# A four-layer graph network kernel on one core: a quarter of the first pass's gathers moved ahead of it, into the sort and the block build

## The reference, cut to what matters

```python
edge_feat = jnp.concatenate([h[src], h[dst]], axis=-1)
messages = _mlp2(edge_feat, msg_W1, msg_b1, msg_W2, msg_b2)
att = jax.nn.sigmoid(_mlp2(edge_feat, att_W1, att_b1, att_W2, att_b2))
weighted = messages * att
aggregated = jax.ops.segment_sum(weighted, dst, num_segments=num_nodes)
combined = jnp.concatenate([h, aggregated], axis=-1)
new_h = _mlp2(combined, upd_W1, upd_b1, upd_W2, upd_b2)
h = new_h + h + global_repr
```

## Time and profile before

| | |
|---|---|
| device time, median of 3 runs | 7433.94 us (7425.34 to 7442.86) |
| span of the profiled execution | 6780.1 us |
| the profiled execution's own time | not given by the page; the median above is 653.8 us over its span |
| busy in the span | PE 5024.0, DVE 3111.1, POOL 2431.9, ACT 1789.9 us |
| gathers of the two attention passes | 1632, 998 ns each in the mean |

### The profile page before, as it was taken

One profiled execution on the slowest core, in us unless ns is written; L12 is line 12 of the kernel. 1 busy time (PEld: TensorE's weight loads), 2 busy tenths in 40 slices (PEclk: granted clock), 3 DMA queues, 4 the chain that ended last, 5 costly groups with the idle time before them and its releaser, 6 DMA issues. The chain is left out here.

```text
span 6780.1 us, 95615 instructions
## 1 busy us (share of the span) xinstructions
PE 5024.0 (74%) x29088; PEld 3414.4 (50%) x29089; DVE 3111.1 (46%) x7292; ACT 1789.9 (26%) x4343; POOL 2431.9 (36%) x2473
## 2 busy tenths in 40 slices
PE   2557767777777777777798999999999997443443
PEld 1435556666665676666544444444444444333333
DVE  6889986666664666666565212112112114111111
ACT  2019983444443444444201001001011012000000
POOL 0000006777773777777100000000000001777776
PEclk7569998999999999999899999999999998555555
DMA  2019984444443444444483553553554524211122
GB/s 79 1 47 328 328 279 133 128 121 125 124 121 80 133 128 130 123 129 126 138 304 131 194 192 133 194 193 131 194 180 146 194 97 167 52 51 51 51 51 55
DMA packets 416540, 942.73 MB, mean 139 GB/s; under 512 B 61857, under 2 KB 272982, under 8 KB 406230
## 3 DMA queue, kind: packets, MB, share of 16 engines
q1 hardware_dynamic: 312150, 672.91, 29.4%
q0 software_dynamic: 104192, 267.02, 14.8%
HBM read 735.13 MB, written 204.56 MB: 139 GB/s over the span
## 5 line engine op out<-in xcount | busy, mean ns | idle before, releaser
L1799 POOL DMA_INDIRECT ring<-rows,stage x1632 | 1629.5, 998 | 1138.4 <-ACT stage L1846 642.0
L1677 POOL DMA_INDIRECT ring<-rows,stage x808 | 792.3, 981 | 2716.8 <-ACT stage L1661 2470.9
L1324 PE MATMUL ps<-strip,trans_part 128*128 128x512 f16 (+1 forms) x8232 | 1606.4, 356 | 23.3 <-DVE trans_part L1241 23.3
L1871 PE MATMUL ps<-here,spread 128*128 x3264 | 949.0, 414 | 545.5 <-DVE spread L1810 283.9
L1324 PEld LDWEIGHTS ps<-strip,trans_part 128*128 128x128 bf16 x8232 | 756.5, 98 | 928.2 <-issue 77.4
L1871 PEld LDWEIGHTS ps<-here,spread 128*128 128x128 f32 x3264 | 569.9, 194 | 662.2 <-issue 615.5
L1829 DVE TENSOR_TENSOR ring<-ring,ps 128x512 f32<-128x512 f32 x816 | 560.6, 687 | 699.3 <-PE ps L1871 540.9
L1728 PE MATMUL ps<-ring,mark 128*128 128x128 f32 x1616 | 414.9, 438 | 612.3 <-DMA ring<-rows,stage 610.7
L1889 PE MATMUL ps<-ring,mark 128*128 128x128 f32 x3264 | 695.0, 300 | 0.0
L1728 PEld LDWEIGHTS ps<-ring,mark 128*128 128x128 f32 x1616 | 357.3, 326 | 669.9 <-issue 669.9
L1233 DVE TENSOR_TENSOR trans<-ps,be 128x512 f32<-128x512 f32 x96 | 66.4, 692 | 1186.4 <-PE ps L1314 1186.4
(11 more groups left out here) (332 smaller groups left out, 5093.7 us busy)
## 6 DMA issues: line engine op xcount, KB each, us to landing
strip<-adj SPq DMA_DIRECT2D x392, 800.0 KB, 4.3
adj<-piece SPq DMA_DIRECT2D x120, 640.0 KB, 4.0
locs<-loc_rows SPq DMA_DIRECT2D x420, 128.0 KB, 3.1
ahead<-ahead_piece SPq DMA_DIRECT2D x125, 320.0 KB, 4.1
back<-back_piece SPq DMA_DIRECT2D x125, 320.0 KB, 4.5
sheet<-ahead SPq DMA_DIRECT2D x25, 1600.0 KB, 7.4
sheet<-back SPq DMA_DIRECT2D x25, 1600.0 KB, 7.2
ring<-rows,stage POOLq DMA_INDIRECT x2440, 2.5
```

The source lines that it names most:

```text
L1324: last = eng.matmul(k.ps[:, b, 0:cols], part[:, (step * NW + w) % TABLES, m, t * D:(t + 1) * D], strip[:, at % RING, c0:c0 + cols], start= ...
L1677: eng.indirect_dma_start(ring[:, t, :], None, rows, bass.IndirectOffsetOnAxis(stage[:, t:t + 1], 0)).then_inc(s_full[q], 16)
L1799: eng.indirect_dma_start(ring[:, t, :], None, rows, bass.IndirectOffsetOnAxis(stage[:, t:t + 1], 0)).then_inc(s_full[q], 16)
L1871: last = eng.matmul(hid[:, j, :], spread[:, q, t * P:(t + 1) * P], here[:, bass.ds(cols[t] * 2, W2)], start=True, stop=True)
```

## The change

- `layer0`'s mean phase and the first step's table become one phase, `first_rows`, which runs between `route` and `adjacency`. It stores both halves of the table to device memory (`rows0`, and `here0`, since no SBUF is free for `here` that early), and `h` as `h0`.
- In the phases of the sort, of decode and of the block build POOL gathers the first tile of each quad, four quads to a group, into six slots that lie in the buffers of `x` and `h` (`Ahead`). Three groups later it stores a group to `early_rows` in device memory with a plain DMA of 512 KB. 40 groups stand in the sort, 4 in decode, 7 in the build: 204 gathers and 51 stores.
- The first attention pass gathers three tiles of each quad. SP brings the fourth from `early_rows` and, at the pass's start, `here`, `h` and `x`. PE waits for `here` before its first `expand`.
- The loop over the two steps is unrolled; the second step still has its table phase and four gathers to a quad. `first_node` becomes the integer tile `src_no`, which is then refilled with the source numbers by one DVE copy.

```diff
+EARLY = NT // QUAD // QUAD
+AFTER_SORT, AFTER_DECODE = 40, 44
...
+                eng.tensor_copy(k.src_no[:, :], k.by_dst[:, 0:NT, D_SRC])
...
+class Ahead:
+    SLOTS, LAG = 6, 3
...
+    def fetch(self, eng):
+        n = self.end - self.first
+        def keep(i):
+            j = i % self.SLOTS
+            eng.wait_ge(self.s_got[j], 16 * QUAD * (i // self.SLOTS + 1))
+            quads = self.k.early[(self.first + i) * QUAD:(self.first + i + 1) * QUAD, :, :]
+            eng.dma_start(quads.rearrange("q p c -> p q c"), self.slots[j]).then_inc(self.s_kept[j], 16)
+
+        for i in range(n):
+            j = i % self.SLOTS
+            if i >= self.SLOTS:
+                eng.wait_ge(self.s_kept[j], 16 * (i // self.SLOTS))
+            for t in range(QUAD):
+                tile = ((self.first + i) * QUAD + t) * QUAD
+                eng.indirect_dma_start(self.slots[j][:, t, :], None, self.k.rows0,
+                                       bass.IndirectOffsetOnAxis(self.k.src_no[:, tile:tile + 1], 0)).then_inc(self.s_got[j], 16)
+            if i >= self.LAG:
+                keep(i - self.LAG)
+        for i in range(max(0, n - self.LAG), n):
+            keep(i)
+        for j in range(min(n, self.SLOTS)):
+            eng.wait_ge(self.s_kept[j], 16 * len(range(j, n, self.SLOTS)))
...
+            for to, of in loads[:1]:
+                eng.dma_start(to, of).then_inc(s_here, 16)
+            for q in range(NQ):
+                fetch(q * QUAD, q)
+                if early is not None:
+                    refill(q, q)
+            for to, of in loads[1:]:
+                eng.dma_start(to, of).then_inc(s_back, 16)
...
-                    for t in range(q * QUAD, (q + 1) * QUAD):
+                    for j in gathered:
+                        t = q * QUAD + j
...
+                    if early is not None:
+                        eng.wait_ge(s_early[q], i * 16 + 16)
...
+            @block.sync
+            def _(eng):
+                eng.dma_start(k.h0, k.h[:, :, :].rearrange("p w d -> p (w d)")).then_inc(s_h, 16)
+                for g in range(NW // G):
+                    eng.wait_ge(s_src, (g + 1) * G)
+                    eng.dma_start(of(k.rows0, g), src_st[:, g % 2, :, :]).then_inc(s_st[g % 2], 16)
+                    eng.wait_ge(s_dst, (g + 1) * G)
+                    eng.dma_start(of(k.here0, g), dst_st[:, g % 2, :, :]).then_inc(s_st[g % 2], 16)
...
-        with nc.Fori(0, 2) as _step:
+        for step in range(2):
+            if step:
...
+        first_rows(k)
```

More of the change, by code:

```diff
@@ L640, in sort_bins @@
     PERM = 4
+    ahead_rows = Ahead(k, 0, AFTER_SORT)
     with nc.Block() as block:
@@ L1748, in open_banks, with attention_pass @@
         eng.matmul(k.ps[:, b, :], k.none[:, 0:P], k.none[:, :], start=True, stop=False, skip_group_check=True)
-def attention_pass(k, own, rows, here, w_att, b_att):
+def attention_pass(k, own, rows, here, w_att, b_att, early=None, loads=()):
     nc = k.nc
@@ L1771, in attention_pass @@
     s_set = k.sem("s_set")
+    s_here, s_back = k.sem("s_here"), k.sem("s_back")
+    gathered = range(QUAD) if early is None else range(1, QUAD)
+    landed = 16 * len(gathered)
     words = k.by_dst
@@ L1780, in fetch, with refill, turn @@
                 eng.dma_start(locs[:, q, :], k.loc_rows[bass.ds(t0, QUAD), :].rearrange("t e -> (t e)").partition_broadcast(P)).then_inc(s_locs[q], 16)
-            for q in range(NQ):
-                fetch(q * QUAD, q)
-            with eng.Fori(0, bodies) as i:
+            def refill(g, q):
+                eng.dma_start(ring[:, q * QUAD, :], early[bass.ds(g, 1), :, :].rearrange("m p c -> p (m c)")).then_inc(s_early[q], 16)
+            def turn(i, more):
                 for q in range(NQ):
@@ L1786, in _ @@
                     fetch(i * in_body + in_body + q * QUAD, q)
+                    if more and early is not None:
+                        eng.wait_ge(s_done, i * NQ + (NQ + q + 1))
+                        refill(i * NQ + (NQ + q), q)
+            for to, of in loads[:1]:
[6 more added lines that the diff above has]
+                eng.dma_start(to, of).then_inc(s_back, 16)
+            with eng.Fori(0, bodies - 1) as i:
+                turn(i, True)
+            turn(bodies - 1, False)
             for q in range(NQ):
                 eng.wait_ge(s_locs[q], 16 * (bodies + 1))
+            eng.wait_ge(s_back, 16 * len(loads[1:])) if loads else None
         @block.gpsimd
@@ L1801, in _ @@
             for q in range(NQ):
-                eng.wait_ge(s_full[q], bodies * 16 * QUAD)
+                eng.wait_ge(s_full[q], bodies * landed)
         @block.vector
@@ L1979, in _ @@
             @block.vector
             def _(eng):
+                for w in range(NW):
+                    g = w // G
+                    eng.wait_ge(s_src, w + 1)
+                    if g >= 2:
+                        eng.wait_ge(s_st[g % 2], 32 * (g // 2))
+                    eng.tensor_tensor(dst_st[:, g % 2, w % G, :], k.ps[:, w % MEAN, HALF:2 * HALF], f.bias1[:, :], ALU.add).then_inc(s_dst, 1)
                 c = Count(eng, s_dve)
@@ new lines, in _, with layer0 @@
+                for j in range(2):
+                    eng.wait_ge(s_st[j], 32 * len(range(j, NW // G, 2)))
+                eng.wait_ge(s_h, 16)
+        k.end_phase()
+def layer0(k, a):
+    f = k.first
+    att_sum = f.att_sum
+    own = ExitStack()
+    with own:
+        here = k.sb("here", [P, NW, 2 * D], F32, own)
+        rows = k.rows0
+        again = [(here[:, :, :], k.here0.rearrange("(w p) d -> p w d", p=P)),
+                 (k.h[:, :, :].rearrange("p w d -> p (w d)"), k.h0), (k.x[:, :, :], a["x"])]
+        for step in range(2):
+            if step:
+                with ExitStack() as inner:
+                    table(k, inner, f.w1, 4 * D, lambda w0, n, st: [(rows[w0 * P:(w0 + n) * P, :].rearrange("(w p) d -> p w d", p=P), st)],
+                          bias=f.bias1, keep=here, shared=2 * D)
@@ L1998, in layer0 @@
             with ExitStack() as inner:
-                table(k, inner, f.w1, 4 * D, lambda w0, n, st: [(rows[w0 * P:(w0 + n) * P, :].rearrange("(w p) d -> p w d", p=P), st)],
-                      bias=f.bias1, keep=here, shared=2 * D)
-            with ExitStack() as inner:
-                attention_pass(k, inner, rows, here.rearrange("p w d -> p (w d)"), f.w_att, f.b_att)
+                attention_pass(k, inner, rows, here.rearrange("p w d -> p (w d)"), f.w_att, f.b_att,
+                               early=None if step else k.early, loads=() if step else again)
```

80 lines of the change are left out of this document (58 added, 22 removed).

## The result

| | before | after |
|---|---|---|
| device time, median (range), same chip | 7431.89 us (7425.34 to 7442.86, 4 runs) | 7198.34 us (7191.01 to 7203.85, 4 runs) |
| ratio after / before | | 0.9679, 95% interval [0.9667, 0.9692] |
| profiled execution | span 6780.1 us, its time unknown | span 7202.1 us, its time 7203.85 us |

The forecast was 7432 us. The kernel became 233.6 us faster.

The account below looks back on a forecast made before the run. It took POOL's gathers, 5.27 us a quad, to bound the first pass, with PE's 5.03 close under; -51 + 6 - 3 + 1 + 8 + 23 + 14 = -2 gave 7432 us, 8-in-10 range 7392 to 7505.

Parts of the forecast that it names:

- The frame: Whole kernel: the profile's span of 6780.1 us plus 653.8 us around it, taken as unchanged.
- The pace: First attention pass: from 5.30 us a quad to PE's 5.03, so -51 us.
- Rival (d): First attention pass falls to POOL's pace, -267 us instead of -51: 7216 us, chance 0.04.
- The start of the pass: First attention pass: PE waits for `here`, first addition near 15 us instead of 8.8, +6 us.
- Mean and table: Moved from before the first pass into one earlier phase: -35.8 us there, +33 for the phase, -3 in all.
- Decode: Decode phase: too short to cover POOL's gathers and stores, with casts slowing POOL, +23 us.
- Build: Block build: gathers and stores load DMA engines already 95.7% busy, +14 us.
- later slack: Block build: 4% of DMA slack later drains the queue but gives ACT no time back.
- The sort: Sort phase: 160 gathers and 40 stores at 1.7 us each slightly outlast its 320 us, +8 us in all.
- Rival (b): POOL's list outlasts the sort through the store's price; at 3.76 us a store 7521 us, chance 0.20.
- rival (c): POOL is locked out while DVE works, the sort growing by about 160 us: 7593 us, chance 0.03.
- rival (a): Sort, decode and build cover better: stores cheap, casts harmless, build's queue absorbed; -26 us, 7408 us, chance 0.27.

Follow-up runs that it names:

- e1: The kernel before, unedited, profiled again on chip 5: 7395.61 us, ratio to before 0.9998.
- e16: The kernel after, unedited, run on chip 13: 6788.11 us, ratio to before 0.9980.
- e4: The kernel after with 48 groups of early gathers in the sort, none in decode, three in the build, on chip 5: 7118.64 us, ratio to before 0.9626.
- e13: The kernel after, second pass with three gathers a quad and a plain DMA from POOL for the fourth tile: 6971.99 us, ratio to before 0.9384.
- e8: The kernel before with gathered rows of 512 bytes instead of 1 KB: 7433.70 us, ratio to before 0.9998.
- e9: The kernel before with 96 rows in each gather instead of 128: 7494.80 us, ratio to before 1.0083.
- e14: The kernel after with the first pass's early tile loaded in four plain DMAs instead of one: 7214.80 us, ratio to before 0.9711.
- e5: The kernel before with PE's column numbers loaded once a pass instead of twice a quad: 7380.49 us, ratio to before 0.9924.
- e7: The kernel of e4 with PE's column numbers loaded once a quad instead of twice, on chip 9: 7171.09 us, ratio to before 0.9637.
- e11: The kernel after with six small POOL memsets ahead of each quad's three gathers in the first pass: 7236.58 us, ratio to before 0.9739.
- e12: The kernel of e4 with two small memsets behind each of a quad's first three gathers in the second pass: 7178.14 us, ratio to before 0.9663.
- e17: The kernel of e4, unedited, run on chip 13: 6768.49 us, ratio to before 0.9958.
- e6: The kernel after with three gathers a quad in both attention passes and no early-tile loads in the loops: 6932.47 us, ratio to before 0.9322.
- e15: The kernel after with two gathers a quad in both attention passes and no early-tile loads in the loops: 6860.94 us, ratio to before 0.9235.

## Why the prediction was wrong

**The frame failed first.** The step was the sentence "what lies around it I take from the median, 7433.9 - 6780.1 = 653.8 us, and leave unchanged". In e1 2 us lie around the span. The 653.8 us stood inside the passes with gathers: 237.9 in the first, 260.2 in the second, 116.4 in the last, 614.5 us in all, and the spans of the two profiles of before differ by 613.3 (the chip of e1 takes 7396 us for the kernel before, not 7434). Of the sum, the term that this spoiled is the pass: I took -51 us for the gathers left out, and in the timed executions it was near -250.

**The pace.** I took 5.30 us a quad before and 5.03 to 5.05 after, -51. On chip 13 that is right: first additions of the quads, first and last one,

```profile
1087.90 0.69 DVE L1904 TENSOR_TENSOR ring<-ring,ps 128x512 f32<-128x512 f32 x1 [0.63 <-PE ps L1946]
...
2113.92 0.69 DVE L1904 TENSOR_TENSOR ring<-ring,ps 128x512 f32<-128x512 f32 x1 [0.85 <-PE ps L1946]
```

(2113.92 - 1087.90)/203 = 5.05 us, and the pass is 40.9 us shorter than in the first profile (I had -51 + 6). In the timed executions the pass of before was not profiled. By e1 and by the second pass after it ran at about 6.5 us a quad, so my estimate for leaving out a gather is 1342.3 - 1091.9 = 250 us. With the +30 us of the other phases that makes -220 of the measured -233.6; the rest is not assigned.

**Rival (d)**, 7216 us with a chance of 0.04, has about the measured size by luck: it is a fall from POOL's pace of 5.27 us a quad to 3.96. The pass fell from about 6.5 to 5.4, and in e1's slow pass the additions waited 4.0 us in all for gathers, so POOL's pace was not its bound. I had argued against it from the earlier trace rows, which are right for their execution.

**The start of the pass.** First addition 1087.99 - 1069.6 = 18.4 us after the phase's start, not 15, before 8.8: +10 for +6. The timeline of DVE after and e16's waits (15.0 us for `locs`) have the reason: the first `spread` waits for `locs`, which stand behind `here` in SP's list.

```profile
1084.93 0.48 DVE L1883 TENSOR_SCALAR spread<-locs,lane 128x512 f32<-128x512 bf16 x1 [15.12 <-issue]
```

**Mean and table:** 31.2 us for the new phase, 35.9 taken away, -4.7 for -3. **Decode:** +21.6 for +23; a gather that meets the casts takes up to 3.29 us. **Build:** +15.0 for +14; PE's waits for ACT's `piece` go from 103.4 to 111.1 us with one of 5.8, DMA share 1.01. Nearly all of it is lost early: POOL's last store there ends 61.7 us into the phase, ACT's 101st instruction starts 87.0 us into it before and 100.5 after, its 401st 328.1 and 342.5. So the later slack gives nothing back, as I had said. The gathers, kernel after, timeline of decode:

```profile
506.37 1.89 POOL L627 DMA_INDIRECT x<-rows,src_no  x1 [0.30 <-issue]
508.57 3.29 POOL L627 DMA_INDIRECT x<-rows,src_no  x1 [0.31 <-issue]
512.16 2.69 POOL L627 DMA_INDIRECT x<-rows,src_no  x1 [0.30 <-issue]
515.16 0.94 POOL L627 DMA_INDIRECT x<-rows,src_no  x1 [0.30 <-issue]
```

**The sort:** +0.2 for +8. The term that was mis-sized is the store: 0.80 us, under the lower end of 0.94 that I gave it. Gathers and stores by line, 177 to 1065 us:

```profile
L627 POOL DMA_INDIRECT x<-rows,src_no x112 | 139.4, 1244 | 95.3 <-PEq L797 61.9 <-issue 33.4
L627 POOL DMA_INDIRECT h<-rows,src_no x92 | 105.5, 1147 | 28.0 <-issue 28.0
L619 POOL DMA_DIRECT2D early_rows<-x x28 | 22.4, 803 | 4.8 <-DMA x<-rows,src_no 4.7
L619 POOL DMA_DIRECT2D early_rows<-h x23 | 18.4, 800 | 0.0
```

1.24 and 1.15 us for a gather are what 0.94 + 0.28 promised. With the cheap store POOL is done 61.9 us before decode, which e4 uses. That many descriptors can be emitted before their cost shows is what the Trainium skill has (DMA: Bandwidth & Descriptors, section Anatomy of one DMA). The traces agree: 0.80 us for 512 rows, 0.58 for 128 (e13). By that sentence I should have taken the sort at 0. Rival (b), a store of over 2 us, and rival (c), POOL locked out, are refuted by the same rows.

**Sum by the phases that the change touches,** with the first pass from chip 13: first pass -40.9, gap before it -1.8, mean and table -4.7, sort +0.2, decode +21.6, build +15.0, together -11 us. The medians on chip 13 differ by 11.7; the forecast had -2 and rival (a) -26, whose cheap stores came true and whose harmless casts did not. That -11 meets 11.7 so closely is partly luck: between the same two traces the untouched second and last pass differ by +25.7 and +15.5 us. The working holds for executions like the one profiled. The time was missed because the profile and the times came from executions that ran differently, and I explained the gap away instead of asking what could be 650 us long.

**What stays open.** By what a fourth gather holds up PE on three of the four chips. It isn't its bytes (e8), its rows (e9), the number of landing signals (e14, and e13 has as many as four gathers) or PE's column loads (e5, e7). POOL's time and the spacing are not excluded: e11 and e12 moved them too little. So one rival stands untested: that PE is held up on these chips once POOL's own list is about as long as PE's 5.03 us a quad. By its busy time and the 0.30 us between two gathers it takes 5.0 to 5.4 us in every slow pass, and at most 4.7 in every quick one on the chips 5, 9 and 15 (estimates from the traces). Enough memsets beside three gathers to pass 5.03 us would decide it. The length alone can't be all, for it is 5.2 to 5.3 us with four gathers in the first profile of before and on chip 13, where nothing is late.

The hold-up reaches PE's own list: in e1's last pass the instructions of PE's sequencer start 0.7, 1.4 or 2.1 us apart from 6304 to 6322 us, where 0.1 is usual for its register operations. Every execution here, the timed ones too, was recorded, so the recording itself could be what holds PE up. The Trainium skill (NOTIFIC — the notification-queue block, section 7.1 Overflow: three behaviours, one of which stalls the engine) knows a mode in which full record queues stall an engine. That would fit the late signals. By the same section it is the alternative to the modes that lose records, so it does not explain the lost ones. No run here shows it, and an execution without records wasn't tried.

## The version that beats both

With 48 groups in the sort (e4, e17) the kernel takes 0.9626 of before on chip 5 and 0.9958 on chip 13, where the change as it is has 0.9980. On chip 13 it is 19.6 us or 0.3% under the kernel after in the medians of twelve executions each, whose ranges overlap (6755.97 to 6784.94 and 6760.7 to 6807.9), and less than the 34 expected: by the two profiles decode gives back 21.6 us and the build 11.3, the sort takes 1.5. The 1057.2 us of e4's first pass are not a gain of its own: on one chip it is 1050.4 in e17 and 1051.9 in e16.

## What to carry to other kernels

Compare the profile's span with its own time, and where that isn't given, with the timed runs. A gap of 9% is no margin around the kernel, it is a sign that the profile shows an execution unlike the timed ones, and a forecast should then carry both as rivals. Count a stretch from barrier to barrier in two traces before explaining anything: phases without gathers agreed to about 1 us here and pointed at the three that didn't.

Moving a quarter of a loop's gathers to stretches where POOL is idle costs little (32 us for 204 gathers and 51 stores, about 5 in the better split). What it brings was 234 us in the first timing and 12 on chip 13, so measure such a change on more than one.

## What the runs showed of the hardware

- A plain DMA of 512 rows of 1 KB to device memory costs POOL 0.80 us to issue (kernel after), one of 128 rows from it 0.58 (e13), a gather of 96 rows 0.95 (e9) and one of 128 rows 0.97 (kernel after) beside other work.
- With gathers on POOL another engine can be held up. On three of four chips PE's semaphores rose up to 6.3 us (kernel after, second pass) after the modelled end of their matmul with four gathers a quad, at most 1.1 us in 95% of the cases with three (e6's second pass), and not late with two (e15). PE's granted clock was 0.81 to 0.87 in the slow attention passes and 0.94 to 0.98 in the others. After the stall at 2997 to 3001 us the matmuls ran at a granted clock of 0.5, 1.2 GHz, from 3001.8 to 3005.2 us. Over the pass PE is busy 912.6 us, against 811.1 in the first pass after, for as many matmuls.
- The same program takes 6800 us on one chip and 7396 to 7434 us on three others.
